# Layer 0's second feed-forward bias added to x by GpSimd instead of by a product on TensorE, with a new order on every engine

## The reference, cut to what matters

```python
h = relu(layernorm(x))                       # z in the kernel
n = layer_norm(h, gamma1, beta1)
a = h + masked_softmax_attention(n, n, n)    # z after its adds
y = layer_norm(a, gamma2, beta2)
x = x + a + gelu(y @ W1 + b1) @ W2 + b2      # b2: 256 values, the same for every node
...
x = x + layer1(relu(layernorm(x)))
```

## Time and profile before

| what | value |
|---|---|
| median of 3 runs | 4241.14 us (4238.12 to 4243.43) |
| the profiled execution, its own time | 4241.92 us |
| its span in the trace | 4240.1 us |
| TensorE busy | 4042.6 us, 95% of the span |
| VectorE busy | 3223.4 us, 76% |
| ScalarE busy | 2166.5 us, 51% |
| GpSimd busy | 408.3 us, 10% |
| mean granted TensorE clock | 0.988 of full speed |

### The profile page before, as it was taken

The page is one execution under the profiler, slowest core; times in us unless marked ns, Lnnn a source line. Parts: engine busy times, 40 slices in busy tenths (PEclk is TensorE's granted clock), DMA queues, the critical chain, the costliest instruction groups (busy, mean ns, idle before and its releaser), DMA issues.

```text
span 4240.1 us, 58963 instructions
## 1 busy us (share of the span) xinstructions
PE 4042.6 (95%) x22884; PEld 1929.7 (46%) x22884; DVE 3223.4 (76%) x6473; ACT 2166.5 (51%) x3361; POOL 408.3 (10%) x469
## 2 busy tenths in 40 slices
PE   5799999999999999999999999999999999999997
PEld 1344444444444444444444444444444444444443
DVE  5677778877778877777877777877778877788854
ACT  3454555544555554555544555544555544555532
POOL 0001011101011101110100110100110100110100
PEclk9999999999999999999999999999999999999998
DMA  3111111111111111111111111112111111211000
GB/s 99 29 42 50 56 37 49 34 53 51 56 36 51 31 53 52 56 36 51 31 52 54 56 35 51 31 51 56 56 32 54 31 51 56 56 31 46 21 31 31
DMA packets 212311, 193.90 MB, mean 46 GB/s; under 512 B 144448, under 2 KB 179008, under 8 KB 203584
## 3 DMA queue, kind: packets, MB, share of 16 engines
q1 hardware_dynamic: 212032, 190.12, 15.3%
HBM read 138.95 MB, written 17.56 MB: 37 GB/s over the span
## 4 chain that ended last, share of the span: by engine, by line
PE 90%; DVE 5%; ACT 4%; DMA 1%; issue 1%; SPq 0%; POOL 0%; POOLq 0%; ACTq 0%; DVEq 0%
PE O L477 12%; PE M L425 11%; PE M L438 10%; PE S L358 6%; PE S L524 6%; PE O L371 6%; PE M L491 6%; PE O L540 6%; PE M L449 6%; PE O L481 5%; PE M L502 3%; PE M L416 3%; PE M L582 3%; PE O L382 2%; ACT PP L625 2%; PE M L398 2%
## 5 line engine op out<-in xcount | busy, mean ns | idle before, releaser
L1014 DVE SCALAR_TENSOR_TENSOR PG<-g,tcg,mT 128x512 f32<-128x512 f32 x1024 | 691.2, 742 | 33.1 <-PE O L481 21.4
L625 ACT ACTIVATE PP<-S,reach 128x1024 f32<-128x1024 f32 x512 | 542.6, 1111 | 318.8 <-PE O L371 114.5
L906 DVE TENSOR_TENSOR PP<-PP,mT 128x1024 f32<-128x1024 f32 x512 | 597.3, 1218 | 16.5 <-ACT PP L625 16.0
L477 PE MATMUL O<-PG,V 128*32 128x512 f32 x4096 | 550.9, 602 | 18.5 <-DVE PG L1014 17.0
L425 PE MATMUL M<-hT,W 128*128 128x512 f32 x1024 | 460.6, 603 | 3.1 <-ACT hT L660 2.8
L438 PE MATMUL M<-W,H 128*128 128x256 f32 x2048 | 459.7, 378 | 0.0
L438 PEld LDWEIGHTS M<-W,H 128*128 128x128 f32 x2048 | 377.3, 189 | 71.7 <-issue 10.6
L1126 POOL TENSOR_SCALAR ve<-mv 128x4 f32<-128x4 f32 x192 | 97.8, 509 | 3197.4 <-DVE mv L864 3197.4
L358 PE MATMUL S<-hT 32*128 32x512 f32 x2048 | 301.3, 658 | 30.8 <-ACT PP L625 29.4
L739 ACT ACTIVATE PP<-S,sh 128x1024 f32<-128x1024 f32 x256 | 272.1, 1118 | 87.5 <-DVE Q L916 49.0
L603 ACT ACTIVATE V<-z,nb,rs 128x256 f32<-128x256 f32 x128 | 76.6, 602 | 467.4 <-DVE nb L896 467.4
(11 more groups left out here) (136 smaller groups left out, 5608.5 us busy)
## 6 DMA issues: line engine op xcount, KB each, us to landing
g<-t_rows SPq DMA_DIRECT2D x64, 1024.0 KB, 4.7
adj<-adj_in SPq DMA_DIRECT2D x32, 1024.0 KB, 5.5
x<-x_in SPq DMA_DIRECT2D x32, 512.0 KB, 4.0
z<-t_rows SPq DMA_DIRECT2D x64, 256.0 KB, 4.0
out<-x SPq DMA_DIRECT2D x32, 512.0 KB, 2.9
W<-w_in SPq DMA_DIRECT2D x1, 3072.0 KB, 13.0
mT<-z SPq DMA_TRANSPOSE x128, 2.5
m<-V SPq DMA_TRANSPOSE x128, 2.5
```

Of the source, the lines that this page charges most:

```text
L477: e.matmul(k.O[0][r:r + 32, :], s.V[:, jt, 64 * hh + 32 * v:64 * hh + 32 * v + 32], p[:, u, :], start=(jt == 0), stop=(jt == NT - 1))
L625: e.activation(p[:, 2 * pair:2 * pair + 2, :], k.S[:, 2 * pair:2 * pair + 2, :], ACT.Exp, bias=k.reach[:, 7:8], scale=SC0).then_inc(k.e0.s ...
L906: e.tensor_tensor(p[:, 2 * pair:2 * pair + 2, :], p[:, 2 * pair:2 * pair + 2, :], s.mT[:, jt:jt + 1, :].to_broadcast([128, 2, N]), ALU.mul ...
L1014: e.scalar_tensor_tensor(out=p[:, u, :], in0=s.T[hh], scalar=s.tcg[:, 1, hh, jt:jt + 1], in1=s.mT[:, jt, :], op0=ALU.max, op1=ALU.mult).th ...
```

## The change

The bias b2 is kept as a full row on all partitions in float32 (`b2row`), and GpSimd adds it to x for all four tiles with one instruction. `resid0` waits for that. The product of ones with b2 goes, and `w2`'s first real product starts the sum. The split of b2 into bfloat16 parts at the start of the program goes too, and GpSimd copies the row once instead.

```diff
@@ Pe.w2
         self.take(f"M{t % 2}", k.w2a.at(b, t))
-        self.wait_ge(k.b_ready, 2)
-        e.matmul(k.M[t % 2][:, 0:256], k.onesb[:, :], k.bias["b2"][:, :], start=True, stop=False)
         for kk in range(8):
             self.wait_ge(*k.gelu.at(b, kk))
             m = e.matmul(k.M[t % 2][:, 0:256], k.H[:, kk, 128 * t:128 * t + 128], w2[:, kk, :],
-                         start=False, stop=(kk == 7))
+                         start=(kk == 0), stop=(kk == 7))
@@ Dve.prep_w
             self.wait_ge(k.b_ready, 1)
+            self.wait_ge(k.b2_kept, 1)
...
-            self.part("b2", k.w("b2"))
@@ Dve.resid0
         self.wait_ge(*k.add[0].at(b, 3))
+        self.wait_ge(*k.xb.at(b, 0))
         e.tensor_tensor(s.x[:, :, :], s.x[:, :, :], s.z[:, :, :], ALU.add).then_inc(k.xx.sem, 1)
@@ Pool
+    def xb(self, b):
+
+        e, k, s = self.e, self.k, self.k.of(b)
+        if b == 0:
+            self.wait_ge(k.w_first, 16)
+            e.tensor_copy(k.b2[:, :], k.w("b2")).then_inc(k.b2_kept, 1)
+            self.wait_ge(k.b2_kept, 1)
+        self.wait_ge(*k.z0.at(b, 3))
+        e.tensor_tensor(s.x[:, :, :], s.x[:, :, :], k.b2[:, None, :].to_broadcast([128, NT, D]),
+                        ALU.add).then_inc(k.xb.sem, 1)
@@ vector_program
-        do.bag(b2, 2, 2)
-        do.bag(b2, 2, 3)
-        do.pa3(b4, 1)
...
+        do.pa3(b3, 1)
+        do.bag(b1, 2, 2)
+        do.bst(b1, 2, 3)
+        do.pj(b2, 2, 0)
+        do.bst(b0, 0, 2)
+        do.bag(b1, 2, 3)
@@ gpsimd_program
-        do.rs(b1, 0)
-        do.rs(b2, 2)
-        do.gmax(b3, 2)
-        do.rs(b1, 1)
-        do.rs(b2, 3)
...
+        do.rs(b2, 0)
+        do.rs(b3, 3)
+        do.rs(b2, 1)
         do.gmax(b3, 1)
         do.rs(b4, 5)
         do.rs(b3, 4)
         do.rs(b2, 2)
         do.gmax(b3, 2)
+        do.xb(b2)
```

More of the change, by code:

```diff
@@ L1327, in tensor_program @@
         do.sc3(b3, 2)
+        do.b2r(b1, 0, 2)
+        do.pv3(b3, 1)
+        do.b2r(b1, 0, 3)
+        do.pj(b2, 2, 0)
+        do.pj(b2, 2, 1)
+        do.sc3(b3, 3)
+        do.pj(b2, 2, 2)
+        do.pj(b2, 2, 3)
+        do.dn3(b3, 0)
+        do.pv3(b3, 2)
+        do.prep_b(b1)
+        do.tt(b1, 0, 0)
+        do.tt(b1, 0, 1)
+        do.pv3(b3, 3)
+        do.w1(b1, 0)
+        do.w1(b1, 1)
+        do.grow(b2, 2)
+        do.dn3(b3, 1)
+        do.w1(b1, 2)
+        do.w1(b1, 3)
+        do.w1(b1, 4)
+        do.w1(b1, 5)
+        do.w1(b1, 6)
+        do.w1(b1, 7)
+        do.w2(b1, 0)
+        do.w2(b1, 1)
+        do.w2(b1, 2)
+        do.w2(b1, 3)
 def scalar_program(do):
@@ L1416, in scalar_program @@
         do.sc3(b3, 3)
+        do.pj(b2, 2, 2)
+        do.ln2(b1, 0)
+        do.pj(b2, 2, 3)
+        do.ln2(b1, 1)
+        do.ln2(b1, 2)
+        do.ln2(b1, 3)
+        do.tt(b1, 0, 0)
+        do.tt(b1, 0, 1)
+        do.gprep(b2, 2)
+        do.w1(b1, 0)
+        do.w1(b1, 1)
+        do.grow(b2, 2)
+        do.w1(b1, 2)
+        do.w1(b1, 3)
+        do.w1(b1, 4)
+        do.w1(b1, 5)
+        do.w1(b1, 6)
+        do.w1(b1, 7)
+        do.ln0(b0, 0)
+        do.out3(b3, 1)
+        do.ln0(b0, 1)
+        do.ln0(b0, 2)
 def vector_program(do):
@@ new lines, in vector_program @@
+        do.b2r(b1, 0, 0)
+        do.rc(b1, 0, 1)
+        do.fin(b1, 0, 0)
+        do.sc3(b3, 1)
+        do.bst(b1, 2, 0)
+        do.pa3(b3, 0)
+        do.b2r(b1, 0, 1)
+        do.rc(b1, 0, 2)
+        do.bag(b1, 2, 0)
+        do.b2r(b1, 0, 2)
+        do.fin(b1, 0, 1)
+        do.bst(b1, 2, 1)
+        do.fin(b1, 0, 2)
+        do.rc(b1, 0, 3)
+        do.bag(b1, 2, 1)
+        do.b2r(b1, 0, 3)
+        do.bst(b1, 2, 2)
+        do.fin(b1, 0, 3)
+        do.pa3(b3, 1)
+        do.bag(b1, 2, 2)
@@ L1557, in vector_program @@
+        do.bst(b1, 2, 3)
+        do.pj(b2, 2, 0)
+        do.bst(b0, 0, 2)
+        do.bag(b1, 2, 3)
+        do.pj(b2, 2, 1)
+        do.sc3(b3, 2)
+        do.pj(b2, 2, 2)
+        do.nb(b1, 2)
+        do.prep_b(b1)
+        do.prep_w(b1)
+        do.bag(b0, 0, 1)
+        do.pj(b2, 2, 3)
+        do.gmax(b2, 2)
+        do.sc3(b3, 3)
+        do.gprep(b2, 2)
+        do.pa3(b3, 2)
+        do.pa3(b3, 3)
+        do.bst(b0, 0, 3)
         do.masks(b0, 0)
-        do.sc3(b3, 0)
-        do.pa3(b3, 0)
@@ L1560, in vector_program @@
-        do.sc3(b3, 1)
-        do.rc(b1, 0, 0)
+        do.bag(b0, 0, 2)
+        do.bag(b0, 0, 3)
+        do.resid0(b1)
         do.nb(b0, 0)
-        do.rc(b1, 0, 1)
-        do.b2r(b1, 0, 0)
-        do.b2r(b1, 0, 1)
-        do.fin(b1, 0, 0)
-        do.bst(b1, 2, 0)
-        do.bag(b1, 2, 0)
-        do.fin(b1, 0, 1)
-        do.rc(b1, 0, 2)
-        do.bst(b1, 2, 1)
-        do.b2r(b1, 0, 2)
-def gpsimd_program(do):
-    for it in range(1, NB + 4):
-        b1, b2, b3, b4 = it - 1, it - 2, it - 3, it - 4
+        do.w2(b1, 0)
@@ new lines, in vector_program @@
+        do.masks(b0, 1)
+        do.bst(b0, 1, 0)
+        do.gvals(b2, 2)
+        do.bag(b0, 1, 0)
+        do.bst(b1, 3, 0)
+        do.w2(b1, 1)
+        do.gw(b2, 2, 0)
+        do.bag(b1, 3, 0)
+        do.w2(b1, 2)
+        do.bst(b1, 3, 1)
+        do.bst(b0, 1, 1)
+        do.bst(b1, 3, 2)
+        do.bst(b0, 1, 2)
+        do.bag(b0, 1, 1)
+        do.bag(b0, 1, 2)
+        do.bag(b1, 3, 1)
+        do.bst(b0, 1, 3)
+        do.bag(b0, 1, 3)
+        do.w2(b1, 3)
+        do.bst(b1, 3, 3)
@@ L1579, in gpsimd_program @@
+        do.bag(b1, 3, 2)
+def gpsimd_program(do):
+    for it in range(2, NB + 4):
+        b2, b3, b4 = it - 2, it - 3, it - 4
+        do.rs(b2, 0)
+        do.rs(b3, 3)
+        do.rs(b2, 1)
         do.gmax(b3, 1)
```

238 lines of the change are left out of this document (73 added, 165 removed).

## The result

The changed kernel takes **4253.1 us** (median of 7 runs, 4249.0 to 4258.1) beside 4239.8 us for the kernel before on the same chip: ratio 1.0031, 95% interval 1.0022 to 1.0040. The forecast was 4251. The profiled execution has a span of 4251.3 us, 11.2 more than before.

What follows compares the result with a forecast made beforehand. TensorE, busy 4042.6 of 4240.1 us, was taken as the bound: 31 periods of its list plus ramps. 4241.9 - 14.1 - 3.1 + 25.7 + 1.0 = 4251.4, forecast 4251 us; own range 4241 to 4260, with rivals 4223 to 4267.

Steps and rivals of the forecast that it cites:

- The product of ones: TensorE's product of ones with b2, issued 128 times: removing it gives back 0.11 us each, 14.1 us (bounds 12.8 to 34.7).
- The start: Batch 0 at program start: `diag` comes later, so statistics number 1 no longer wait behind the DMA transposes; 3.1 us gained once.
- The addition: GpSimd's addition of b2 to x: 1.1 to 3.2 us, covered by VectorE's wait for the first `w2` bank, so 0.
- Statistics number 2: Later last `bag` delays `rs`, GpSimd's reduction and gelu, so TensorE's `grow` starts 0.83 us later a period: +25.7 us (0 to 37).
- The rest of the order: TensorE's waits for PP and PG could go, one for `b2r`'s normalized tile comes: 0, bounds -0.6 and +0.5 us a period.
- The end: Batch 31, TensorE's wait for layer 1 or 2 relu: four instructions now stand between a `bag` and its `nb`; +1 us once.
- The first rival: GpSimd's chain is in time and TensorE keeps its gain: 4225.7 us, or down to 4208 without PP and PG waits; chance 0.30.

Runs made afterwards that it cites:

- The old order without it: Kernel before with all lists in the old order, only the product of ones exchanged for GpSimd's addition of b2 behind the second reduction: 4227.2 us.
- `diag` alone: Old order with GpSimd's addition behind the second reduction (4227.2 us), only `diag` moved between the two `wo` steps: 4223.3 us.
- the run with `xb` ahead: Old order with GpSimd's addition of b2 moved ahead of `rs` of statistics number 2, against 4227.2 us with it behind the reduction: 4294.9 us.
- The version with the early bag: Changed kernel with the last `bag` of layer 0's statistics number 2 put back ahead of layer 3's addition into Q on VectorE: 4207.1 us.

## Why the prediction was right, and where only its sum was

- *The product of ones*, -14.1: right. The old order without it is 0.40 us a period shorter, 12.4 us, and 13.1 by the ratio.
- *The start*, -3.1: the mechanism right (3.3 us for `diag` alone), the term short by 2 us, whose source was not found; 5.3 in all.
- *The addition*, 0: right, and shown four times (without it in either order, fourfold, and by the waits). It takes 2.34 us, inside the bounds of 1.1 to 3.2, where I had put it at the upper end; the change of code ahead of it takes 7.5 us and not 5.8, and the cover held that, too. I had priced only GpSimd's time, though; what it can cost VectorE I had not asked, and the run with `xb` ahead shows that to be the larger price, 68 us, in another place.
- *Statistics number 2*, +25.7: place and mechanism right, as the earlier trace rows had them, and the size too small: 1.43 x 31 = 44 us, above even the upper bound of 37. That the wait at `grow` is 0.77 us where I had 0.83 is a coincidence. I had meant 0.83 as the lateness of the whole chain; it is 1.44, and TensorE spends 0.61 of it at the transposes of y, a branch from `rs` that I had not followed. The chain was mis-sized in two links. `rs` ends 6.87 us behind `rc` where I had 6.48: it takes 3.44 us and not 3.2, since its first instruction was held over both multiplications (2.32 us; in the old order 1.11, over one large instruction), and the bag and the hand-over to GpSimd make up the rest. And I took the chain's slack as 0.3 us from the end of one gelu; ScalarE's end and TensorE's `grow` are never closer than 0.14 us, and in the old order the median distance is 0.28, so the slack was 0.14. 1.51 us of lateness, less 0.14, and 0.07 by which the reduction's start behind `rs` differs, make the 1.44.
- *The rest of the order*, 0: wrong. It gains 0.50 us a period, 15.5 us, near the low bound of -0.6 that I had written down. The waits for PP and PG went, and only the one for V came; I had let them cancel without weighing them.
- *The end*, +1: nothing to be seen (192.8 us before and after), but nothing refuted either: from the last batch's `w2` to the end it is 190 to 195 us in the kernels of the table, so 1 us doesn't stand out.

So errors of both signs met, against the times as they came out: 18.6 us too little for the bag and 1.7 too much gain for the product, against 15.5 for the rest of the order, 2.2 at the start and 1 at the end. The sum, 4251, was closer than its terms, and that was luck. The first rival (GpSimd's chain in time, 4225.7 or down to 4208) is what the kernel does as soon as the bag stands where it did: 4207.

## What to carry to other kernels

When a step is late, list everything that hangs on it, on every engine, and follow each chain to where it ends. The waits along the way are not prices to be added up or compared with the forecast one by one: a later wait shows only what the earlier ones have left, and the latest chain sets the loss. A small instruction of GpSimd costs what the large VectorE instructions beside it make of it: put such a step (statistics, a power, a bias) where VectorE does single-input work or stands still, and order the two so that the small one goes first. And when a change brings an exchange of work and a new order together, run the exchange in the old order: here it was worth 13 us, and the new order took 26 back, through one misplaced instruction that cost 46.

## What the runs showed of the hardware

- The hold between VectorE and GpSimd goes both ways: 0.18 us became 2.33 on VectorE, over one addition of GpSimd's, and 0.23 became 2.32 on GpSimd, over two multiplications that stand back to back. GpSimd's power, issued in the same way behind the start of the first of two, took 2.00 and 2.08 us instead of 1.04, so it was held over one. What decides whether GpSimd gets in between two is not shown.
- GpSimd's change of code costs more on the way back: 5.8 to 6.3 us ahead of the reduction, 6.7 to 7.8 (7.1 in the mean of 31) ahead of the addition behind it.
- TensorE's clock fell to 1.2 GHz for a moment in some periods, always in the stretch with `b2r`, L348 and the first scores. The version with the early bag, in steps of 1 us (busy TensorE, loads, VectorE, ScalarE, GpSimd, granted clock, DMA share, GB/s):
```profile
2658.00:2659.00 1.00, 0.73 (x7) 0.67 (x8) 1.00 (x5) 0.00 (x0) 0.00 (x0) 1.00 1.02 342
2659.00:2660.00 1.00, 0.98 (x7) 0.62 (x5) 1.00 (x5) 0.65 (x1) 0.00 (x0) 0.78 0.03 9
2660.00:2661.00 1.00, 1.00 (x6) 0.52 (x8) 1.00 (x3) 0.13 (x1) 0.00 (x0) 0.50 0.41 32
2661.00:2662.00 1.00, 1.00 (x8) 0.00 (x0) 1.00 (x3) 0.00 (x0) 0.00 (x0) 0.50 0.64 167
2662.00:2663.00 1.00, 1.00 (x8) 0.20 (x8) 1.00 (x3) 0.60 (x1) 0.00 (x0) 0.51 1.09 351
```
  It fell behind the waits for `b2r`'s banks (TensorE busy for 0.73 of a microsecond), and was back at 2.4 GHz in the slice after the last one shown. The same waits were there in periods without a fall (busy for 0.70 in the microsecond from 2405 on, granted clock 1.00), so they alone don't explain it. Between 300 and 4000 us this happened ten times in that run, seven times in the changed kernel and five times before. It cost nothing: `w2` starts at 2620.05, 2746.73 and 2873.40 across two such falls and at 2113.35, 2240.02 and 2366.70 without one, 126.67 or 126.68 us apart in all four. TensorE does lose time: L477 starts 42.19 us behind `w2` across the first of these falls and 41.20 without one. But at the next scores it is 0.33 us behind (47.81 against 47.48), and the last of that comes off a later wait for V (0.40 us instead of 0.53); behind it both are at 59.57. VectorE is busy for the whole of each microsecond shown, which fits TensorE going at its pace there.
